# Another order of the source digits, source fields and bank clears in the set-up of a two-layer graph kernel, with the low-digit one-hots made on GpSimd

## The chip, the cores and the metric

The kernel runs on one core of one Trainium2 chip. The metric is the device time of one execution in microseconds (us). All numbers of the kernel before are from three timed runs and one further execution that the hardware profiler recorded.

Engines are called by these names in the rows: PE is TensorE's matrix multiply, PEld its weight load, DVE is VectorE, ACT is ScalarE, POOL is GpSimd, SP is SyncE, and a q behind a name is the queue of that engine (SPq issues most of the transfers).

## The reference

Two graph layers over 12,500 nodes with 128 features and 212,500 edges (100,000 drawn pairs in both directions and one loop for each node), sorted by target. Both have the form x = x + layer(relu(layernorm(x))).

```python
h = jnp.maximum(_layernorm(x, axis=-1), 0.0)
# layer 0
src_h = h[src] @ W_msg.T + b_msg
msg = src_h + edge_embed[jnp.clip(edge_type, 0, 8)]
messages = segment_sum(msg, dst)
x = x + gru_cell(messages, h)
h = jnp.maximum(_layernorm(x, axis=-1), 0.0)
# layer 1
agg = segment_sum(h[dst], src)
z = ((1.0 + eps) * h + agg) @ W1.T + b1
z = relu(batchnorm(z))
x = x + z @ W2.T + b2
```

Layer 0 sums over the targets, and layer 1 sums over the sources, though the edges are sorted by target. So the kernel must know for every edge where it would stand in an order by source.

## The kernel before

The nodes are cut into 98 blocks of 128, the edges into 1,664 tiles of 128. The program has one hand-written instruction list for each engine, and semaphores between them.

**Set-up.** It does three things side by side. (1) The first norm and the message table: 14 turns (LN_TURNS) of 7 blocks each. In a turn SP loads x (`load_x`), VectorE makes the statistics (`norm_stats`, `norm_scale`), ScalarE takes a root (`deviation`) and applies the norm (`norm0`), TensorE transposes (`hT`), ScalarE moves the result (`keep_hT`), TensorE multiplies by W_msg (`messages`), ScalarE moves it (`table_rows`), and SP writes it to the table in DRAM. Four buffers hold the loads. (2) The packed edges: target, source and type are packed into one word, written to DRAM, and read back with one tile in each column (semaphore `packed_in`). (3) The histogram of the sources: the high digit (13 values) and the low digit (8 values) of every edge's source block are turned into one-hot rows of bf16, in 13 pieces of 128 tiles (DPIECES), and TensorE multiplies the two one-hots of a piece (`digit_counts`, 16 multiplications) into bank 6. `digit_fields` takes the digits out of the packed words, and `digit_onehots(i)` makes the one-hots of piece i, in two buffers; piece i waits until TensorE has counted piece i-2. DIG_AT is the turn at which VectorE begins with the digits: from that turn on each turn also makes one piece, and the rest follow behind the last turn. TensorE counts a piece behind the transposes and messages of its turn, in the order of its list.

**From the histogram to the first gather.** When all 13 pieces are counted, VectorE reads bank 6, takes the source numbers out of the packed words, TensorE transposes them, ScalarE copies them to `srcI` (the first four of twelve `fields_moved`), and GpSimd copies 128 columns of them as offsets (`place_idx`) and begins to gather rows of the message table, one indirect transfer for each tile of 128 edges. Before its first gather GpSimd also waits until the message table is written (`tab_out`).

**The rest of the set-up on VectorE.** It makes the targets within a block (LOC), which ScalarE copies as fields 5 to 8; the first rows of each source block (`base_s`); the types (VAL, fields 9 to 12); the rows of `lastrow`, by which SP pads the last tiles; then `sblkE` and `skeyE`, block and key of each source, from `srcI`; and, at the head of layer 0, the first one-hots. Then `lastrow_set` lets SP write the padding rows.

**ScalarE behind the fields.** It clears the 7 fields' room and the rest of the sums Y (`zero_y`, in two parts; the second waits until VectorE has read the fields), then the two banks for the type counts (`counts_zero`) and four banks for the sums (`agg_zero`).

**Layer 0.** GpSimd issues 1,664 gathers into a ring of 8 slots of 4 tiles. SP relays: for each slot it tells TensorE that the rows have come (`tiles_in`) and, from the fourth on, tells GpSimd that a slot is free (`slot_free`), when the sums that read it are done. Between its first relays SP issues the padding rows and waits for each before the next (`pad_tiles`). TensorE multiplies each tile by a one-hot of its targets, VectorE adds the banks to Y. Then come the gated cell, layer 1 with 1,664 indirect scatters on GpSimd, and the last multiplications.

## Time and profile before

| | us |
|---|---|
| three timed runs, median | 4887.57 |
| lowest and highest | 4886.05 and 4891.22 |
| the profiled execution | 4883.31 |
| its span, first to last instruction | 4881.0 |
| GpSimd busy in the span | 3442.0 (71%) |
| TensorE busy | 3759.2 (77%) |
| VectorE busy | 2671.9 (55%) |
| ScalarE busy | 1613.8 (33%) |

The rows of the profile are read as follows. A row of the timeline has the start and the duration in us, the engine, the line in the kernel before, the operation, what it writes and what it reads, the shapes, and how many such instructions were merged; in brackets stand the idle time of the engine just before it and what ended that. A group of instructions has the total busy time, the mean in ns of one, and the idle time before all of them. The profiled execution is 4.26 us shorter than the median of the timed runs, and 2.31 us of it lie outside of the span.

### The profile page before, as it was taken

How to read it: one execution, taken by the hardware profiler on the slowest of the kernel's cores; microseconds unless marked ns; L12 is line 12 of the kernel's file. 1: busy time of each engine (PE TensorE's matmuls, PEld its weight loads, DVE VectorE, ACT ScalarE, POOL GpSimd, SP SyncE). 2: the span in 40 equal slices, each digit the busy share in tenths (PEclk: the TensorE clock that was granted, in tenths of full speed). 3: DMA queues.
4: the chain of work that ended last, by engine and by line, in shares of the span. 5: the costliest groups of instructions: out<-in, count | busy, mean ns of one | idle time of the engine just before them, and what ended most of it. 6: DMA issues, size and time to landing. Idle time of an engine off the chain costs nothing.

```text
span 4881.0 us, 93192 instructions
## 1 busy us (share of the span) xinstructions
PE 3759.2 (77%) x22928; PEld 2659.4 (54%) x23224; DVE 2671.9 (55%) x4808; ACT 1613.8 (33%) x3340; POOL 3442.0 (71%) x3576
## 2 busy tenths in 40 slices
PE   4698888888888888888787777777677775677457
PEld 3455555555555555556654444444466674667456
DVE  7777777777777777756821111111255552555267
ACT  4433333333333333333432222222222222222266
POOL 1577777777777777774167777777777777777763
PEclk8799988989899888999998999988888886788689
DMA  5332333333333221222222222222355553555365
GB/s 151 98 82 80 80 81 81 81 80 81 81 80 81 64 53 53 53 52 55 75 92 81 81 85 81 81 86 81 125 182 177 186 185 125 167 174 185 103 240 159
DMA packets 316351, 514.65 MB, mean 105 GB/s; under 512 B 73350, under 2 KB 231737, under 8 KB 300189
## 3 DMA queue, kind: packets, MB, share of 16 engines
q1 hardware_dynamic: 209245, 286.59, 18.6%
q0 software_dynamic: 106944, 226.05, 15.7%
q8 instruction: 83, 1.36, 0.1%
q14 instruction: 79, 0.65, 0.0%
HBM read 331.72 MB, written 180.64 MB: 105 GB/s over the span
## 4 chain that ended last, share of the span: by engine, by line
POOL 66%; issue 24%; PE 4%; DVE 2%; DMA 1%; POOLq 1%; ACT 1%; SPq 0%; ACTq 0%; DVEq 0%
POOL rows_by_src L692 34%; POOL sb_ring L662 31%; PE ps L1777 2%; DMA rows_by_src<-sb_cf 0%; PE ps L1797 0%; PE ps L1789 0%; POOL sb_oh L677 0%; DVE sb_stepE L966 0%; POOLq L157 0%; DMA rows_by_src<-sb_ring,sb_idxslot 0%; DVE sb_smalls L945 0%; ACT sb_ring L731 0%; DVE sb_stepE L969 0%; POOLq L689 0%; POOLq L153 0%
## 5 line engine op out<-in xcount | busy, mean ns | idle before, releaser
L692 POOL DMA_INDIRECT rows_by_src<-sb_ring,sb_idxslot x1664 | 1693.6, 1018 | 537.6 <-issue 503.8
L662 POOL DMA_INDIRECT sb_ring<-msg_table,sb_idxslot x1664 | 1584.9, 952 | 516.6 <-issue 504.1
L1593 PE MATMUL ps<-sb_zeros_b 128*128 128x512 bf16 x5465 | 1461.8, 416 | 105.2 <-issue 94.0
L1593 PEld LDWEIGHTS ps<-sb_zeros_b 128*128 128x128 bf16 x5760 | 580.8, 106 | 726.5 <-issue 284.2
L1733 PE MATMUL ps<-sb_H,sb_oh 128*128 x3520 | 616.1, 338 | 459.0 <-ACT ps L867 275.3
L1733 PEld LDWEIGHTS ps<-sb_H,sb_oh 128*128 128x128 f32 x3520 | 567.1, 245 | 562.3 <-issue 547.8
L1373 DVE TENSOR_SCALAR sb_oh<-sb_oh,sb_cf 128x512 f32<-128x512 bf16 x440 | 208.4, 501 | 1081.0 <-PE ps L1733 977.8
L791 ACT CAST sb_counts<-ps 54x512 bf16<-54x512 f32 x440 | 254.3, 578 | 1307.4 <-PE ps L1615 1294.8
L873 ACT CAST sb_ring<-sb_skeyE 128x4 f32 (+1 forms) x416 | 82.2, 198 | 1594.1 <-DMA rows_by_src<-sb_ring,sb_idxslot 1592.2
L1601 PEld LDWEIGHTS ps<-sb_ring,sb_oh 128*128 128x128 f32 x3520 | 504.5, 201 | 159.3 <-issue 95.9
L1601 PE MATMUL ps<-sb_ring,sb_oh 128*128 x3520 | 529.1, 292 | 41.4 <-SPq L476 41.1
L1230 DVE TENSOR_TENSOR sb_Y<-sb_Y,ps 128x512 f32 x440 | 300.8, 684 | 370.8 <-PE ps L1623 365.9
L1615 PE MATMUL ps<-sb_oh,sb_toh 128*54 128x128 bf16 x1760 | 244.8, 234 | 230.3 <-issue 214.4
L1198 DVE TENSOR_REDUCE sb_blks<-sb_blk1h 128x99 bf16<-128x396 bf16 x417 | 342.3, 821 | 0.0
L1217 DVE TENSOR_TENSOR sb_ranked<-ps,sb_blk1h 128x396 f32<-128x396 f32 x416 | 234.8, 564 | 183.6 <-PE ps L312 175.0
L1615 PEld LDWEIGHTS ps<-sb_oh,sb_toh 128*54 128x54 bf16 x1760 | 129.0, 106 | 326.5 <-issue 250.0
L1391 DVE TENSOR_TENSOR sb_Y<-sb_Y,ps 128x512 f32 x376 | 257.0, 684 | 69.0 <-PE ps L1746 57.1
L1381 DVE TENSOR_TENSOR sb_stepE<-sb_stepE,sb_cf 128x512 f32<-128x512 f32 x188 | 125.2, 686 | 285.6 <-PE ps L1746 285.4
L786 ACT CAST ps<-sb_zeros_b 54x512 f32<-54x512 bf16 x442 | 257.4, 582 | 14.1
L798 ACT CAST ps<-sb_zeros_b 128x512 f32<-128x512 bf16 x438 | 253.0, 578 | 12.3 <-DVE sb_Y L1230 12.3
L875 ACT COPY sb_ring<-ps 128x512 f32<-128x512 f32 x416 | 240.7, 579 | 36.6 <-PE ps L1733 36.6
L867 ACT CAST ps<-sb_zeros_b 128x512 f32<-128x512 bf16 x420 | 247.3, 589 | 13.3
(239 smaller groups left out, 4348.1 us busy)
## 6 DMA issues: line engine op xcount, KB each, us to landing
sb_stepE<-rows_by_src SPq DMA_DIRECT2D x110, 1088.0 KB
sb_oh<-step_targets SPq DMA_DIRECT2D x110, 512.0 KB, 3.9
rows_by_src<-sb_cf SPq DMA_DIRECT2D x588, 68.0 KB
sb_ring<-msg_table,sb_idxslot POOLq DMA_INDIRECT x1664
rows_by_src<-sb_ring,sb_idxslot POOLq DMA_INDIRECT x1664
sb_ring<-rows_by_src SPq DMA_DIRECT2D x15, 1088.0 KB, 5.1
msg_table<-sb_oh SPq DMA_DIRECT2D x14, 448.0 KB, 3.3
sb_oh<-in_x SPq DMA_DIRECT2D x49, 128.0 KB, 2.1
```

The lines of the kernel that those rows point to most:

```text
L662: pool.indirect_dma_start(out=ring[:, r * G + q, 0:F], out_offset=None, in_=table_d[:, :], in_offset=bass.IndirectOffsetOnAxis(ap=idxslot[ ...
L692: pool.indirect_dma_start(out=rows_d[:, :], out_offset=bass.IndirectOffsetOnAxis(ap=idxslot[:, h, g * G + q:g * G + q + 1], axis=0), in_=r ...
L786: return nc.scalar.copy(bank(5 + k)[0:TROWS, :], zeros_b[0:TROWS, :])
L791: nc.scalar.copy(counts[:, k, :], bank(5 + k)[0:TROWS, :]).then_inc(S("counts_moved"), 1)
L798: nc.scalar.copy(bank(1 + (g + 2) % G), zeros_b[:, :]).then_inc(S("agg_zero"), 1)
L1198: vs.tensor_reduce(blks[:, slot, :], own_blocks(slot).rearrange("p q b -> p b q"), axis=AX.X, op=ALU.add) \
L1230: vs.tensor_tensor(yb, yb, bank(1 + g), ALU.add).then_inc(S("agg_added"), 1)
L1391: vs.tensor_tensor(yb, yb, bank(GPC + g), ALU.add).then_inc(S("bank_free"), 1)
L1593: mm(o, zeros_b[:, 0:P], zeros_b[:, :], start=False, stop=True, skip_group_check=True)
L1601: mm(o, oh[:, k, s, :], ringf[:, ds(tile, F)], start=False, stop=True, skip_group_check=True)
L1615: m = mm(o, type_cols(k, s, q * HALVES // G), ohb[:, k, s, 1:2 * P:2], start=False, stop=True, skip_group_check=True)
L1733: m = mm(picked_ps[:, ds(slot, P)], pick[g][:, q * P:(q + 1) * P], H[:, ds(off, P)], start=False, stop=True, skip_group_check=True)
```

## The change

Four edits, all in the set-up.

1. DIG_AT goes from 3 to 6: VectorE begins with the digits three turns later, and TensorE's counts follow. Five pieces instead of two lie behind TensorE's last turn.
2. The low-digit one-hots move from VectorE (one TENSOR_TENSOR of 128x1024 for each piece) to GpSimd (eight TENSOR_SCALAR of 128x128 for each piece, one for each digit value, comparing with a constant and writing every eighth element), 104 instructions in all. They stand behind the 14 gathers of step tiles and ahead of the waits on the message table. `digits_set` starts them, and `hist_hi` and `hist_lo` take the place of `hist_oh`. The low digits are made in another buffer (`lo_dig`).
3. `sblkE` and `skeyE` are made ahead of the wait on fields 5 to 8, instead of behind `lastrow`.
4. ScalarE clears the count banks and the sum banks ahead of Y.

```diff
-DIG_AT = 3
+DIG_AT = 6
...
+            pool.wait_ge(S("digits_set"), 1)
+            for i in range(DPIECES):
+                wait(pool, "hist_ps", i - 1)
+                a = i * DPIECE
+                for h in range(NLO):
+                    o = nc.gpsimd.tensor_scalar(lo_oh[i % 2].rearrange("p (c h) -> p c h", h=NLO)[:, :, h],
+                                                lo_b[:, a:a + DPIECE], float(h), None, ALU.is_equal)
+                o.then_inc(S("hist_lo"), 1)
...
-            zero_y(3 * SW, Y.shape[1])
-            act.wait_ge(S("fields_read"), 1)
-            act.wait_ge(S("loc_out"), 16)
-            zero_y(0, 3 * SW).then_inc(S("y_zero"), 1)
...
             for g in range(G):
                 nc.scalar.copy(bank(1 + g), zeros_b[:, :]).then_inc(S("agg_zero"), 1)
+
+            zero_y(3 * SW, Y.shape[1])
+            act.wait_ge(S("fields_read"), 1)
+            act.wait_ge(S("loc_out"), 16)
+            zero_y(0, 3 * SW).then_inc(S("y_zero"), 1)
...
-                                 iota_b[:, 0:NHI].unsqueeze(1).to_broadcast([P, DPIECE, NHI]), ALU.is_equal)
-                vs.tensor_tensor(lo_oh[i % 2].rearrange("p (c h) -> p c h", h=NLO),
-                                 lo_b[:, a:a + DPIECE].unsqueeze(2).to_broadcast([P, DPIECE, NLO]),
-                                 iota_b[:, 0:NLO].unsqueeze(1).to_broadcast([P, DPIECE, NLO]), ALU.is_equal) \
-                    .then_inc(S("hist_oh"), 1)
+                                 iota_b[:, 0:NHI].unsqueeze(1).to_broadcast([P, DPIECE, NHI]), ALU.is_equal) \
+                    .then_inc(S("hist_hi"), 1)
...
-                link(vs.tensor_copy(hi_b, packed))
-                link(vs.tensor_scalar(packed, fldi[1][:, 0:TILES], 25, NLO - 1, ALU.logical_shift_right, ALU.bitwise_and))
-                link(vs.tensor_copy(lo_b, packed))
+                vs.tensor_copy(hi_b, packed)
+                link(vs.tensor_scalar(lo_dig, fldi[1][:, 0:TILES], 25, NLO - 1, ALU.logical_shift_right, ALU.bitwise_and))
+                vs.tensor_copy(lo_b, lo_dig).then_inc(S("digits_set"), 1)
+                dve.wait_ge(S("digits_set"), 1)
...
+            tmp = fldi[2][:, 0:TILES]
+            vs.memset(sblkE[:, TILES:TILES + G], 0.0)
+            link(vs.tensor_scalar(tmp, srcI, 7, None, ALU.logical_shift_right))
+            link(vs.tensor_copy(sblkE[:, 0:TILES], tmp))
+            link(vs.tensor_scalar(tmp, srcI, P - 1, None, ALU.bitwise_and))
+            link(vs.tensor_copy(skeyE[:, :], tmp))
 
             dve.wait_ge(S("starts_ps_s"), 1)
             dve.wait_ge(S("fields_moved"), 8)
...
-                pe.wait_ge(S("hist_oh"), i + 1)
+                pe.wait_ge(S("hist_hi"), i + 1)
+                pe.wait_ge(S("hist_lo"), i + 1)
```

On VectorE, where the digits begin: in the kernel before, the digits (L1095 to L1098) follow the statistics of turn 4, and a piece is one high and one low one-hot (L966, L969).

```order
L945 BN_STATS sb_smalls<-sb_ring 128x6 x7
L950 BN_AGGR sb_smalls<-sb_smalls 128x2 x7
L1095 TENSOR_SCALAR sb_Y<-sb_Y 128x1664
L1096 CAST sb_Y<-sb_Y 128x1664
L1097 TENSOR_SCALAR sb_Y<-sb_Y 128x1664
L1098 CAST sb_Y<-sb_Y 128x1664
L966 TENSOR_TENSOR sb_stepE<-sb_Y,sb_iota_b 128x1664
L969 TENSOR_TENSOR sb_stepE<-sb_Y,sb_iota_b 128x1024
L957 RECIPROCAL sb_smalls<-sb_smalls 128x7
```

In the changed kernel (whose lines are numbered about 10 higher) they follow the statistics of turn 7.

```order
L956 BN_STATS sb_smalls<-sb_stepE 128x6 x7
L961 BN_AGGR sb_smalls<-sb_smalls 128x2 x7
L1103 TENSOR_SCALAR sb_Y<-sb_Y 128x1664
L1104 CAST sb_Y<-sb_Y 128x1664
L1105 TENSOR_SCALAR sb_Y<-sb_Y 128x1664
L1106 CAST sb_Y<-sb_Y 128x1664
L977 TENSOR_TENSOR sb_stepE<-sb_Y,sb_iota_b 128x1664
L968 RECIPROCAL sb_smalls<-sb_smalls 128x7
```

The four digit instructions stand six statistics rows later, and the row of 128x1024 is gone from every piece.

On GpSimd, between the gathers of step tiles and the first offsets of layer 0, before:

```order
L619 COMPARE_AND_BRANCH
L617 UNCONDITIONAL_BRANCH
L635 DMA sb_Y<-packed_edges,sb_smalls 128x128 x14
L652 COPY sb_idxslot<-sb_stepE 128x128
L662 DMA sb_ring<-msg_table,sb_idxslot 128x128 x68
```

and now:

```order
L636 DMA sb_Y<-packed_edges,sb_smalls 128x128 x14
L645 ISA
L645 TENSOR_SCALAR sb_stepE<-sb_Y 128x128 x104
L662 COPY sb_idxslot<-sb_stepE 128x128
L672 DMA sb_ring<-msg_table,sb_idxslot 128x128 x68
```

The 104 comparisons stand directly ahead of the first gathers.

On VectorE behind the targets (the last cast of LOC), before:

```order
L1142 CAST sb_Y<-sb_Y 128x1792
L1149 CAST sb_Y<-ps 128x198
L1150 CAST sb_Y<-ps 128x99
L1151 TENSOR_SCALAR sb_Y<-sb_Y 128x297
L1153 TENSOR_TENSOR sb_Y<-sb_Y,sb_cf 128x297
```

and now:

```order
L1151 CAST sb_Y<-sb_Y 128x1792
L1154 MEMSET sb_sblkE 128x2
L1155 TENSOR_SCALAR sb_Y<-sb_stepE 128x1664
L1156 CAST sb_sblkE<-sb_Y 128x1664
L1157 TENSOR_SCALAR sb_Y<-sb_stepE 128x1664
L1158 CAST sb_skeyE<-sb_Y 128x1664
L1164 CAST sb_Y<-ps 128x198
```

The five instructions on the sources stand in front of the wait that L1149 (now L1164) begins with.

## Rows read from the trace of the kernel before

**Rows 1.** The page: busy time of each engine, and the chain that ended last.

```profile
PE 3759.2 (77%) x22928; PEld 2659.4 (54%) x23224; DVE 2671.9 (55%) x4808; ACT 1613.8 (33%) x3340; POOL 3442.0 (71%) x3576
...
POOL 66%; issue 24%; PE 4%; DVE 2%; DMA 1%; POOLq 1%; ACT 1%; SPq 0%; ACTq 0%; DVEq 0%
```

**Rows 2.** Groups of instructions on GpSimd: the scatters and the gathers.

```profile
L692 POOL DMA_INDIRECT rows_by_src<-sb_ring,sb_idxslot x1664 | 1693.6, 1018 | 537.6 <-issue 503.8 <-ACT sb_ring L875 33.8
L662 POOL DMA_INDIRECT sb_ring<-msg_table,sb_idxslot x1664 | 1584.9, 952 | 516.6 <-issue 504.1 <-SPq L480 11.7 <-POOL sb_idxslot L652 0.8
```

**Rows 3.** Timeline, 61 to 70 us: SP's queue and VectorE at the digits.

```profile
61.31 0.25 SPq L427 DMA_DIRECT2D sb_rowtab<-step_tables  x1
65.22 1.03 DVE L1095 TENSOR_SCALAR sb_Y<-sb_Y 128x1664 int32<-128x1664 int32 x1 [12.54 <-DMA sb_Y<-packed_edges]
...
69.47 1.89 DVE L966 TENSOR_TENSOR sb_stepE<-sb_Y,sb_iota_b 128x1664 bf16<-128x1664 bf16 x1
```

**Rows 4.** The line that loads x: time from issue to landing.

```profile
DMA to landing us min/median/max: 4.4/5.7/10.2
```

**Rows 5.** Timeline, 111 to 117 us: one turn on VectorE, and ScalarE's next norm.

```profile
111.33 0.19 DVE L957 RECIPROCAL sb_smalls<-sb_smalls 128x7 f32<-128x7 f32 x1
...
113.81 1.86 DVE L966 TENSOR_TENSOR sb_stepE<-sb_Y,sb_iota_b 128x1664 bf16<-128x1664 bf16 x1
...
115.59 1.22 DVE L969 TENSOR_TENSOR sb_stepE<-sb_Y,sb_iota_b 128x1024 bf16<-128x1024 bf16 x1
...
116.72 0.20 DVE L957 RECIPROCAL sb_smalls<-sb_smalls 128x7 f32<-128x7 f32 x1
...
117.15 2.80 ACT L731 ACTIVATE sb_ring<-sb_ring,sb_smalls 128x128 f32<-128x128 f32 x7 [0.71 <-DVE sb_smalls L959]
```

**Rows 6.** Timeline, 131 to 142 us: the last one-hot and the first gather.

```profile
131.60 1.22 DVE L969 TENSOR_TENSOR sb_stepE<-sb_Y,sb_iota_b 128x1024 bf16<-128x1024 bf16 x1
...
141.45 1.01 POOL L662 DMA_INDIRECT sb_ring<-msg_table,sb_idxslot  x1 [0.78 <-POOL sb_idxslot L652]
```

**Rows 7.** GpSimd's key one-hots at the kernel's end: ns min, median, max of one.

```profile
L711 POOL TENSOR_SCALAR sb_oh<-sb_cf,sb_ring x75: 593/601/1318, 4674.4 to 4817.6; 128x128 f32<-128x128 f32 x75
```

**Rows 8.** GpSimd's copies of offsets, in the same form.

```profile
L652 POOL COPY sb_idxslot<-sb_stepE x13: 288/299/306, 140.4 to 2004.5; 128x128 int32 x10, 128x128 int32<-128x128 int32 x3
```

**Rows 9.** Timeline of GpSimd, 4677 to 4698 us: two groups of five key one-hots.

```profile
4677.98 2.91 POOL L711 TENSOR_SCALAR sb_oh<-sb_cf,sb_ring 128x128 f32<-128x128 f32 x5 [0.29 <-PE ps L1777]
...
4693.41 3.87 POOL L711 TENSOR_SCALAR sb_oh<-sb_cf,sb_ring 128x128 f32<-128x128 f32 x5 [2.50 <-PE ps L1777]
```

**Rows 10.** Timeline of VectorE under the second of them.

```profile
4693.98 0.85 DVE L1427 TENSOR_TENSOR sb_H<-sb_H,sb_b2b 128x640 f32 x1
4695.10 0.56 DVE L1416 TENSOR_TENSOR sb_oh<-sb_ring,sb_cf 128x384 f32<-128x384 f32 x1 [0.26 <-issue]
...
4696.27 0.47 DVE L1416 TENSOR_TENSOR sb_oh<-sb_ring,sb_cf 128x256 f32<-128x256 f32 x1
```

**Rows 11.** Timeline, 155 to 189 us: VectorE, ScalarE and SP behind the first gather.

```profile
155.11 0.36 DVE L1149 CAST sb_Y<-ps 128x198 int32<-128x198 f32 x1 [3.88 <-ACT sb_stepE L770]
...
162.43 1.03 DVE L1175 TENSOR_SCALAR sb_Y<-sb_stepE 128x1664 int32<-128x1664 int32 x1
...
162.77 6.18 ACT L775 CAST sb_Y<-sb_zeros_b 128x7168 f32<-128x7168 bf16 x1
...
171.23 6.73 SPq L455 DMA_DIRECT2D rows_by_src<-sb_cf  x4
...
174.96 2.14 ACT L804 CAST ps<-sb_zeros_b 128x512 f32<-128x512 bf16 x4
...
188.33 0.69 DVE L1230 TENSOR_TENSOR sb_Y<-sb_Y,ps 128x512 f32 x1 [9.59 <-PE ps L1623]
```

**Rows 12.** Timeline of GpSimd, 188 to 201 us: the 32nd and the 33rd gather.

```profile
188.28 0.94 POOL L662 DMA_INDIRECT sb_ring<-msg_table,sb_idxslot  x1 [0.31 <-issue]
200.02 0.94 POOL L662 DMA_INDIRECT sb_ring<-msg_table,sb_idxslot  x1 [10.80 <-SPq L480]
```

7 lines of the change are left out of this document (1 added, 6 removed).

## The prediction, made before the changed kernel ran

> **What bounds the kernel now.** I read the page's busy times and its chain first. TensorE has more busy time than GpSimd, but the chain that ended last lies 66% on GpSimd, and the 24% called issue are mostly the gaps between its transfers [rows 1]. The groups of GpSimd say why: 1,664 gathers of 952 ns with 0.30 us between them (504.1 us of issue), and the same again for the scatters; in the whole of layer 0 GpSimd waited only 11.7 us for a free slot [rows 2]. So layer 0 ends about 1664 x 1.25 = 2080 us behind the moment from which GpSimd can gather without a stop, and what the set-up loses or saves ahead of that moment goes to the end one for one. Nothing later runs by an absolute date, so I count only the shift of that moment.
>
> That moment is not the first gather (141.45 [rows 6]). The 32 tiles of the ring are issued by 188.28, the 33rd could go at 188.28 + 1.25 = 189.5, and it goes at 200.02, released by SP's relay [rows 12]. The relay hangs on the padding rows that SP starts at 171.23, when VectorE has set `lastrow_set` [rows 11]: 28.8 us from there to the 33rd gather, with padding transfers one behind the other. The ring's date has 10.5 us of room, the relay's has none. Both dates come from the histogram: the first through SRC, TensorE and ScalarE, the second through VectorE's list. If the histogram ends D later, both move by D. So the shift at the end is D plus what the list between histogram and `lastrow_set` gains or loses.
>
> **Edit 3, the source fields.** VectorE is idle for 3.88 us in front of L1149, waiting for ScalarE's copies; the block that moves there is a small clear and four instructions of 1.03 us with hardly a gap, 4.3 us, and began at 162.43 [rows 11]. It reads `srcI`, which has been there since the first gather. In its new place it covers the idle time and passes it by 0.4 us. Removed 4.3, added 0.4: **3.9 us less** on the way to `lastrow_set`. What is late next is the ring's own date; of its 10.5 us of room 6.6 are left, so the whole 3.9 counts.
>
> **Edit 4, ScalarE's clears.** All the clears ended at 174.96 + 2.14 = 177.1 [rows 11]. In the new order the banks are clear first and Y last, at about the same time, for the work is the same and the wait on `fields_read` is met earlier. Y is first needed by VectorE's add at 188.33 [rows 11], in the new kernel 3.9 earlier, 184.4 on the old scale. Cover of 7 us, so nothing; the cleared banks let TensorE start its first counts earlier, and then it waits for the relay all the same. Without that cover each us of late clear would cost one. Nothing.
>
> **Edit 1, the digits three turns later.** Before, VectorE stood idle 12.54 us for the packed words and started the digits at 65.22, the first one-hot at 69.47; they take 4.25 us [rows 3]. Now it goes on with the norm meanwhile. The digits follow the statistics of turn 7. These need x of turn 7, and SP issues that load behind the table loads that end at 61.31 + 0.25, and one table write: at about 62.0. Its landing takes 5.7 us in the median [rows 4]: 67.7. Statistics take 2.1 (of the 2.48 from 111.33 to 113.81, without the scale's 0.38 [rows 5]): 69.8. Digits: 4.25. So `digits_set` comes at **74.0**, 4.5 us later than the first one-hot began before, but with three turns more of the norm done.
>
> From there a turn would be quick: it took 5.39 us (111.33 to 116.72), of which the low one-hot is 1.13 (115.59 to 116.72), so VectorE needs 4.26; ScalarE waited 0.71 in it, so ScalarE needs 4.68 [rows 5]. Were GpSimd free of cost, the histogram would end thus: first high one-hot 75.9, seven turns of 4.7 to 108.8, five pieces of 1.89 behind them to 118.3, against 131.60 + 1.22 = 132.8 before [rows 6]. D would be -14.5. That is the best case.
>
> **Edit 2, GpSimd's 104 comparisons.** They are in a row with the histogram: the last piece cannot be counted before they are done. A piece costs 8d + L: d is the time of one comparison, L what VectorE takes from GpSimd.
>
> d has no row. The nearest above is GpSimd's key one-hot: the same operation on as many elements, but with a scalar from a tensor for each partition and 32-bit data; 601 ns in the median [rows 7], and 2.91 / 5 = 0.58 us from start to start [rows 9]. The nearest below is its copy of 128 elements, 299 ns [rows 8], with neither comparison nor scalar. The new instruction has the comparison, a constant in the place of the tensor's scalar, and bf16 written with a step of eight. I see no reason to set it at either end and take the middle, **d = 0.44**, with 0.30 and 0.58 for the range.
>
> L: five key one-hots took 2.91 us alone and 3.87 when VectorE ran three TENSOR_TENSORs with both inputs in SBUF, 0.85 + 0.56 + 0.47 us [rows 9, 10]. That is 0.96 lost in 1.88, or each of them less 0.3. The high one-hot is such an instruction too and takes 1.86 [rows 5]: L = 1.86 - 0.3 = **1.56**. Bounds: 0, and 1.86.
>
> The Trainium skill (SBUF — State Buffer, "Who interferes with whom") says that a VectorE instruction with two SBUF inputs and a GpSimd instruction that reads SBUF exclude each other for the whole instruction. The rows agree in kind and fall 0.3 us short of it in size; by the rule alone the sum below would be 13 x 0.3 = 3.9 us longer.
>
> Sum: 74.0 + 13 x (8 x 0.44 + 1.56) = 74.0 + 66.0 = 140.0. A piece of 5.08 us is longer than ScalarE's 4.68, so GpSimd sets the pace, and the norm's turns follow it, because TensorE counts a piece between two turns. The message table is done well ahead: five pieces, 25 us, lie behind its last turn. D = 140.0 - 132.8 = +7.2. **Net: 7.2 - 3.9 = +3.3 us.** The profiled execution would go from 4883.31 to 4886.6. The median lies 4.26 above the profiled one, and I keep that distance: 4887.57 + 3.3 = 4890.9. A measurement of this kernel can tell about 0.2%, 9.8 us, from no change.
>
> **Rivals.**
> - *GpSimd's comparisons cost as much as the key one-hots* (slower). With d = 0.58 and L = 1.56: 13 x 6.20 = 80.6, end 154.6, D = +21.8, net +17.9: 4905.5. With L = 1.86 net +21.8: 4909.4. It decides from 8d + L = 4.82 on (d = 0.41), and is over 0.2% from 5.58 on (d = 0.50). For it: the same operation and element count [rows 7]. Against it: no scalar to fetch, half the bytes.
> - *GpSimd is hidden under the turns* (faster). If 8d + L stays under 4.7, the norm's turns set the pace and D is -14.5, net -18.4: 4869.2. That wants d under 0.39 with L = 1.56, or a small L. Over 0.2% faster is reached at 8d + L = 4.07. For it: the copy's 0.30 [rows 8] would give 3.96 a piece.
> - *The move does not reach the end.* If something else than the histogram sets the 33rd gather, as the ring's own date, all that is left is noise about 4887.6. Against it: 10.80 us of idle time that SP ended [rows 12].
>
> The Trainium skill (GPSIMD Engine Reference, 3.1) gives about 1.8 cycles for an element at 1.2 GHz in the best case: an estimate of 0.19 us for 128 elements and the dispatch on top, near the copy's end. By it the second rival would come true. The key one-hots of this trace take three times as long, so it holds here for the copy at most, and no run yet shows which way the new instruction goes.
>
> **How the numbers follow.** Chances: the forecast, a piece between 4.1 and 5.6 us, 0.44; slower rival 0.34; faster rival 0.20; no reach 0.02, which counts as within. So faster by over 0.2% 0.20, within 0.46, slower 0.34. The best case's 4869.2 asks that every turn runs at ScalarE's pace and loads never wait; I leave the last part of it out, and take the slower rival with both its values of L in: 4875 to 4909.
>
> **What would show it right or wrong.** In the changed kernel's timeline: `digits_set` at 74, the 104 comparisons with start to start near 0.44 us and a stop of about 1.6 at each high one-hot; the last count near 141; the first gather near 149; VectorE's source block directly behind LOC with no idle time of 3.9 in front of L1164; the 33rd gather near 203, still released by SP. Wrong would be a comparison at 0.3 or at 0.6, VectorE's one-hots not holding GpSimd at all, x loads that bring `digits_set` past 78, or a first add of VectorE that waits for Y.

## The result, and the profile after

| | kernel before | changed kernel |
|---|---|---|
| median, us (range) | 4891.22 (4886.05 to 4894.47) | 4921.63 (4911.25 to 4931.17) |
| ratio, 95% interval | | 1.0062 (1.0048 to 1.0077) |
| profiled execution: time / span | 4883.31 / 4881.0 | 4922.07 / 4919.6 |
| 104 comparisons: first start to last end | | 74.46 to 186.54 |
| first gather | 141.45 | 195.89 |
| 33rd gather | 200.02 | 250.40 |
| last gather / first scatter / last scatter | 2244.9 / 2456.1 / 4658.0 | 2294.5 / 2503.3 / 4695.9 |

The change costs 0.6%, some 30 us. The forecast was 4890.9 with a range up to 4909: the sign of the small loss was right, its size was not, and the time is outside the range.

GpSimd's groups in the changed kernel (line, operation, count, then busy us and mean ns, then idle time before them and who ended it), and one line's summary (ns min/median/max):

```profile
L702 POOL DMA_INDIRECT rows_by_src<-sb_ring,sb_idxslot x1664 | 1684.1, 1012 | 536.5 <-issue 503.5 <-ACT sb_ring L886 32.9
L672 POOL DMA_INDIRECT sb_ring<-msg_table,sb_idxslot x1664 | 1584.0, 952 | 512.7 <-issue 502.6 <-SPq L481 9.3 <-POOL sb_idxslot L662 0.8
L645 POOL TENSOR_SCALAR sb_stepE<-sb_Y 128x128 bf16<-128x128 bf16 x104 | 107.9, 1189 | 24.6 <-DVE sb_Y L1106 20.4
```

```profile
L645 POOL TENSOR_SCALAR sb_stepE<-sb_Y x104: 984/987/2685, 74.5 to 185.6; 128x128 bf16<-128x128 bf16 x104
```

The gathers are what they were, the scatters 9.5 us shorter in all [rows 2]; the third group is new. Its timeline, with the gathers behind it:

```profile
74.46 112.08 POOL L645 TENSOR_SCALAR sb_stepE<-sb_Y 128x128 bf16<-128x128 bf16 x104 [20.40 <-DVE sb_Y L1106]
...
195.89 1.20 POOL L672 DMA_INDIRECT sb_ring<-msg_table,sb_idxslot  x1 [0.81 <-POOL sb_idxslot L662]
```

```profile
242.63 0.94 POOL L672 DMA_INDIRECT sb_ring<-msg_table,sb_idxslot  x1 [0.30 <-issue]
250.40 0.94 POOL L672 DMA_INDIRECT sb_ring<-msg_table,sb_idxslot  x1 [6.82 <-SPq L481]
```

The comparisons start where the forecast put them (74.0), but take 112.08 us in place of 66.0: 8.62 us a piece, not 5.08. The histogram's last piece ends at 186.54, where before it ended at 132.82 [rows 6]: D is +53.7, not +7.2. Who waited for them (engine and line, whom it waited for, us in total, times, longest):

```profile
PE ps L1534 <- POOL sb_stepE L645: 62.8, 13, 9.3
DVE sb_stepE L977 <- PE ps L1534: 60.3, 11, 6.8
```

The whole histogram now walks at GpSimd's pace. VectorE's high one-hots stand 8.67 us apart, with 6.8 us idle before each, and its first step behind the histogram waits 13.87:

```profile
163.85 1.89 DVE L977 TENSOR_TENSOR sb_stepE<-sb_Y,sb_iota_b 128x1664 bf16<-128x1664 bf16 x1 [6.78 <-PE ps L1534]
172.52 1.89 DVE L977 TENSOR_TENSOR sb_stepE<-sb_Y,sb_iota_b 128x1664 bf16<-128x1664 bf16 x1 [6.78 <-PE ps L1534]
```

```profile
188.28 0.36 DVE L1122 TENSOR_TENSOR sb_ranked<-ps,sb_cf 104x192 f32<-104x192 f32 x1 [13.87 <-PE ps L1534]
```

Edits 3 and 4 did what the forecast said. The source block fills VectorE's idle time, and the line that had waited 3.88 us [rows 11] now follows it with no wait:

```profile
208.90 1.03 DVE L1158 CAST sb_skeyE<-sb_Y 128x1664 bf16<-128x1664 int32 x1
210.04 0.36 DVE L1164 CAST sb_Y<-ps 128x198 int32<-128x198 f32 x1
```

ScalarE clears the banks, then Y; the padding rows start at 222.14, and VectorE's first add into Y waits for TensorE, long after Y is clear (232.2):

```profile
218.89 2.13 ACT L809 CAST ps<-sb_zeros_b 128x512 f32<-128x512 bf16 x4
220.97 6.16 ACT L785 CAST sb_Y<-sb_zeros_b 128x7168 f32<-128x7168 bf16 x1
...
231.81 0.40 ACT L787 CAST sb_Y<-sb_zeros_b 128x256 f32<-128x256 bf16 x1
```

```profile
222.14 7.56 SPq L456 DMA_DIRECT2D rows_by_src<-sb_cf  x4
```

```profile
240.71 0.69 DVE L1239 TENSOR_TENSOR sb_Y<-sb_Y,ps 128x512 f32 x1 [14.39 <-PE ps L1633]
```

So +53.7 and -3.9 should make +49.8 at the 33rd gather, and it came +50.4. From here on the account has a second hole: the last gather is +49.6, but the last scatter only +37.9, and the medians differ by 30. The scatters of the kernel before and of the changed one (ns min/median/max, first and last start):

```profile
L692 POOL DMA_INDIRECT rows_by_src<-sb_ring,sb_idxslot x1664: 963/967/3222, 2456.1 to 4658.0; - x185
L702 POOL DMA_INDIRECT rows_by_src<-sb_ring,sb_idxslot x1664: 954/958/3212, 2503.3 to 4695.9; - x185
```

Each is 9 ns shorter, at the least and in the median. Two questions: why is a comparison so dear, and where do some 15 to 20 us come back?

### The profile page after: what moved, and what is told of

Its sections match the earlier page's. It is cut to its first block, busy times and chain, and to the rows that moved or that the text cites. A ratio compares the mean times of both kernels' runs of the same rounds, so it can differ in the third digit from the quotient of the medians.

```text
span 4919.6 us, 93236 instructions
## 1 busy us (share of the span) xinstructions
PE 3767.8 (77%) x22928; PEld 2675.2 (54%) x23224; DVE 2661.0 (54%) x4795; ACT 1616.1 (33%) x3340; POOL 3535.9 (72%) x3680
## 4 chain that ended last, share of the span: by engine, by line
POOL 67%; issue 24%; PE 4%; DMA 2%; DVE 1%; POOLq 1%; SPq 1%; ACT 1%; ACTq 0%; DVEq 0%
POOL rows_by_src L702 34%; POOL sb_ring L672 30%; PE ps L1787 3%; POOL sb_stepE L645 2%; DMA rows_by_src<-sb_cf 1%; PE ps L1807 0%; PE ps L1799 0%; DMA rows_by_src<-sb_ring,sb_idxslot 0%; POOL sb_oh L687 0%; SPq L463 0%; PE ps L1603 0%; POOLq L157 0%; POOLq L699 0%; POOLq L153 0%; SPq L464 0%
## 5 line engine op out<-in xcount | busy, mean ns | idle before, releaser
L1625 PE MATMUL ps<-sb_oh,sb_toh 128*54 128x128 bf16 x1760 | 244.9, 234 | 223.0 <-issue 214.3
```

The costliest lines, as they stand in the source:

```text
L1625: m = mm(o, type_cols(k, s, q * HALVES // G), ohb[:, k, s, 1:2 * P:2], start=False, stop=True, skip_group_check=True)
```

## Experiments on the price of a comparison

**Taken apart at the end of GpSimd's list.** The kernel before, with comparisons and copies added behind its last key one-hots:

```diff
+            for h in range(8):
+                gt.tensor_scalar(d8[0][:, :, h], src, float(h), None, EQ)      # bf16, step 8
+            for k in range(4):
+                gt.tensor_scalar(ringf[:, 1024 + k * P:1024 + (k + 1) * P], iota_f, iota_p, None, EQ)
...
+            for k in range(4):
+                gt.tensor_scalar(tb[:, 3072 + k * P:3072 + (k + 1) * P], src, 3.0, None, EQ)
+            for h in range(8):
+                gt.tensor_scalar(d8[1][:, :, h], src, 7.0 if h < 4 else 0.0, None, EQ)
...
+            for k in range(3):
+                gt.tensor_scalar(rb[:, k * 512:(k + 1) * 512], skeyE[:, 0:512], 3.0, None, EQ)
```

> The kernel before with a row of small instructions at the end of GpSimd's list, behind its last key one-hots, where VectorE runs nothing with two SBUF inputs. In order: 8 comparisons exactly as in the changed kernel (bf16, constants 0 to 7, columns 0 to 7 with step 8); 4 as the key one-hots (f32, scalar from a tensor, dense); 4 f32 dense with a constant; 4 bf16 dense with a constant; 8 bf16 with step 8, where the constant is 7 for columns 0 to 3 and 0 for columns 4 to 7; 4 f32 with step 8; 3 bf16 dense of 512 elements; 8 copies bf16 with step 8; 4 copies bf16 dense. Their results are used by nothing. Theory A (the write with a step makes the cost): bf16 dense 0.6 us or less, both step-8 groups near 1.05 from start to start, the f32 one with step 8 too. Theory B (a comparison with a constant or in bf16 costs it): bf16 dense near 1.05 too, and the copies at 0.3 in either pattern. Either way the first group shows whether columns 4 to 7 cost more than 0 to 3 (0.60 against 1.05 in the changed kernel), and the fifth whether that goes with the column or with the constant.

GpSimd's timeline:

```profile
4832.11 7.08 POOL L723 TENSOR_SCALAR sb_oh<-sb_skeyE 128x128 bf16<-128x128 bf16 x8 [7.34 <-PE ps L1814]
4839.27 2.35 POOL L725 TENSOR_SCALAR sb_ring<-sb_cf 128x128 f32<-128x128 f32 x4
4841.59 2.02 POOL L727 TENSOR_SCALAR sb_ring<-sb_cf 128x128 f32<-128x128 f32 x4
4843.56 2.02 POOL L729 TENSOR_SCALAR sb_oh<-sb_skeyE 128x128 bf16<-128x128 bf16 x4
4845.64 7.07 POOL L731 TENSOR_SCALAR sb_oh<-sb_skeyE 128x128 bf16<-128x128 bf16 x8
...
4854.35 4.46 POOL L735 TENSOR_SCALAR sb_ring<-sb_skeyE 128x512 bf16<-128x512 bf16 x3
```

Eight of the change's comparisons, with no other engine near, take 7.1 us: 0.88 each, as in the changed kernel. The key one-hot's own form takes 0.58 here (L725: 2.32 to the next group, four of them), a constant in place of the tensor's scalar 0.49 (L727), and bf16 in place of float32 changes nothing as long as the values are written side by side (L729: 0.49 between starts). So type and scalar are innocent; the write with a step of eight is part of it. Singly, the starts of L723 are 0.60 apart for constants 0 to 3, 1.10 from 3 to 4, and 1.06 from 4 on. L731 exchanged the constants over the columns, and the gaps went with the constants, not with the columns.

**Constant, data or place in the list.** Other constants and data in the same spot: eight with 3, eight with 7, four side by side with 7, eight from another row with 7 and 3, four of step 4 and two of step 2, eight that ask "not less than".

```diff
+            for h in range(8):
+                gt.tensor_scalar(d8[0][:, :, h], src, 3.0, None, EQ)
+            for h in range(8):
+                gt.tensor_scalar(d8[1][:, :, h], src, 7.0, None, EQ)
+            for k in range(4):
+                gt.tensor_scalar(rb[:, k * P:(k + 1) * P], src, 7.0, None, EQ)
+            for h in range(8):
+                gt.tensor_scalar(d8[2][:, :, h], iota_f, 7.0 if h < 4 else 3.0, None, EQ)
...
```

> The kernel before with 38 comparisons of 128 elements at the end of GpSimd's list, after its last key one-hots: nothing else waits for them but the end of the program. The first probe left open what makes a comparison that writes bf16 at every eighth place take 0.60 us or 1.06 us: constants 0 to 3 gave 0.60 and constants 4 to 7 gave 1.06, in whatever column. Eight with constant 3 (all columns), eight with constant 7 (all columns), four dense ones with constant 7, eight of step 8 from a float32 row with constants 7 and 3, four of step 4 and two of step 2 with 7 and 3, eight that ask for 'not less than' 7 and 3. Theory C (the constant itself): constant 3 gives 0.60 eight times and constant 7 gives 1.06 eight times, and 7 is dearer than 3 in the step-8 groups with other data and other operation too. Theory M (what the data hold, the number of ones written): the float32 row, in which each value stands once in every partition, gives one time for 7 and 3 alike, and 'not less than' turns the order round. Theory P (the place in the list, four cheap and four dear ones): both groups of eight show four and four. The dense ones with constant 7: 0.49 if the step is needed for the dear form, about 0.9 if not. Time: that of the kernel before plus about 25 us.

```profile
6272.95 5.34 POOL L724 TENSOR_SCALAR sb_oh<-sb_skeyE 128x128 bf16<-128x128 bf16 x8 [7.34 <-PE ps L1811]
6278.35 8.39 POOL L726 TENSOR_SCALAR sb_oh<-sb_skeyE 128x128 bf16<-128x128 bf16 x8
6286.80 2.30 POOL L728 TENSOR_SCALAR sb_ring<-sb_skeyE 128x128 bf16<-128x128 bf16 x4
```

and single instructions at the passage from constant 7 to constant 3 and on to the next group, which begins with 7:

```profile
6292.33 0.99 POOL L730 TENSOR_SCALAR sb_oh<-sb_cf 128x128 bf16<-128x128 f32 x1
6293.38 0.99 POOL L730 TENSOR_SCALAR sb_oh<-sb_cf 128x128 bf16<-128x128 f32 x1
6293.98 0.99 POOL L730 TENSOR_SCALAR sb_oh<-sb_cf 128x128 bf16<-128x128 f32 x1
...
6295.18 1.04 POOL L730 TENSOR_SCALAR sb_oh<-sb_cf 128x128 bf16<-128x128 f32 x1
6296.28 0.70 POOL L732 TENSOR_SCALAR sb_ring<-sb_skeyE 128x128 bf16<-128x128 bf16 x1
```

Theory C holds: eight with constant 3 take 5.34 us, eight with constant 7 take 8.39, whatever they are compared with; the float32 row and "not less than" show the same gaps. Data and place are out. The lines also say what the expected text had not seen: one comparison of step 8 takes 0.99 to 1.15 us whatever its constant; with constants up to 3 the next one starts before it has ended, 0.60 behind, and if either of two neighbours is a 7 it starts only after the end. The step sets the size: with 7 the gap is 0.59 side by side (with 3 it was 0.49, so a 7 costs 0.10 even there), 0.63 at step 2, 0.77 at step 4 and 1.06 at step 8. Why a constant should matter is not explained by anything here. (This ran on another chip, on which the whole kernel is slower; more on that below. GpSimd's instructions take the same time on it.)

**The same comparisons in place, written side by side.** GpSimd writes each comparison's 128 values as neighbours, and TensorE reads them with a step instead:

```diff
-                    o = nc.gpsimd.tensor_scalar(lo_oh[i % 2].rearrange("p (c h) -> p c h", h=NLO)[:, :, h],
+                    o = nc.gpsimd.tensor_scalar(lo_oh[i % 2][:, h * DPIECE:(h + 1) * DPIECE],
...
-                           lo_oh[i % 2][:, a * DW:(a + 1) * DW], start=False, stop=True, skip_group_check=True)
+                           lo_oh[i % 2].rearrange("p (h c) -> p c h", h=NLO)[:, a * DCOLS:(a + 1) * DCOLS, :],
+                           start=False, stop=True, skip_group_check=True)
```

> The changed kernel, but GpSimd writes each comparison densely (128 elements of one digit value behind the other) and TensorE reads them with a step of 128; the counts are the same. Theory A (the write with a step): a comparison about 0.6 us, a piece 8 x 0.6 + 1.6 = 6.4 us in the place of 8.62, the last comparison near 158 in the place of 186.5, and 28 us faster than the changed kernel, so about at the time of before. Theory B (the instruction itself costs 1 us): no difference from the changed kernel, some 30 us slower than before.

```profile
75.05 79.27 POOL L645 TENSOR_SCALAR sb_stepE<-sb_Y 128x128 bf16<-128x128 bf16 x104 [21.09 <-DVE sb_Y L1106]
...
164.08 1.20 POOL L672 DMA_INDIRECT sb_ring<-msg_table,sb_idxslot  x1 [0.81 <-POOL sb_idxslot L662]
```

79.27 us in place of 112.08: 6.10 a piece. The step alone costs the change 33 us. Yet the 33rd gather is still 18.9 us later than in the first profile of the kernel before (218.91), and the time, 4888.2 against 4892.3 (ratio 0.9995, 0.9986 to 1.0005), shows none of it: the second hole again.

## Experiments on the other edits

**Edit 3 alone** (the source block moved in the kernel before, as in the diff of the change):

> The kernel before with the block of source fields in its new place and nothing else. If the relay's date sets the 33rd gather: first gather unchanged at 141.5, 33rd gather at 196.1 in the place of 200.0, 3.9 us faster (0.08%). If the ring's own date or something behind it sets the pace, the 33rd gather stays at 200 and there is no difference.

**Edits 1, 3 and 4, without edit 2** (VectorE makes both one-hots):

```diff
-            pool.wait_ge(S("digits_set"), 1)
-            for i in range(DPIECES):
...
+                vs.tensor_tensor(lo_oh[i % 2].rearrange("p (c h) -> p c h", h=NLO),
+                                 lo_b[:, a:a + DPIECE].unsqueeze(2).to_broadcast([P, DPIECE, NLO]),
+                                 iota_b[:, 0:NLO].unsqueeze(1).to_broadcast([P, DPIECE, NLO]), ALU.is_equal) \
+                    .then_inc(S("hist_oh"), 1)
```

> The changed kernel with the low one-hots back on VectorE (edits 1, 3 and 4 alone). If GpSimd's comparisons are the whole loss: digits_set at 74, seven turns of 5.4 us and five pieces of 3.1 behind them, last low one-hot near 130 against 132.8 before, the 33rd gather near 193 (200.0 minus 2.8 minus 3.9), and 7 us faster than before. If the later start of the digits costs by itself (rival): last low one-hot at 140 or later and no gain.

The first gives 4885.19 (0.9989, 0.9979 to 0.9999), the second 4885.06 (0.9981, 0.9972 to 0.9991), against 4892.3. Their 33rd gathers stand at 194.16 and 195.02, 5.9 and 5.0 us earlier than in the first profile of the kernel before. But that date moves by itself. On the same chip as these two, the kernel before with the comparisons at its end, whose set-up is untouched, had its 33rd gather here:

```profile
197.93 0.95 POOL L662 DMA_INDIRECT sb_ring<-msg_table,sb_idxslot  x1 [9.41 <-SPq L480]
```

Against it the two are 3.8 and 2.9 us earlier. So edit 3 is worth its 3.9 us, and edits 1 and 4 add nothing that shows, in the date or in the time, whose intervals overlap: the change is a small gain with its second edit left out.

**The digits two turns later than before, one earlier than in the change** (`DIG_AT = 5`, the rest as in the last one):

> Edits 3 and 4 with both one-hots on VectorE and the digits before the norm scale of turn 5 (DIG_AT 5): one turn earlier than in the kernel with edits 1, 3 and 4, where the last low one-hot came at 129.4 and the first gather at 139.9. The one-hots then start where the load of the packed rows has just landed. Expected: last low one-hot at 127 to 129, first gather at 138 to 140, and the median 5 to 10 us under the kernel before, 0 to 3 under that with DIG_AT 6. Rival (the wait for the load stalls VectorE's norm turns): 0 to 3 over it.

```profile
65.13 1.03 DVE L1097 TENSOR_SCALAR sb_Y<-sb_Y 128x1664 int32<-128x1664 int32 x1 [0.32 <-DMA sb_Y<-packed_edges]
```

The packed words have just landed when VectorE comes to the digits (0.32 us idle in place of 12.54 [rows 3]), and the norm of two more turns is done. The 33rd gather comes at 192.18, 4882.87 against 4889.86 (0.9984, 0.9975 to 0.9993). The last low one-hot starts at 126.18 and the first gather at 136.67, against 129.40 and 139.88 with `DIG_AT` at 6 (on another chip): by these dates the best place for the digits is where their data arrive, and the change had passed it by a turn. The two times do not tell them apart.

**Edit 1 undone in the changed kernel:**

```diff
-DIG_AT = 6
+DIG_AT = 3
```

> The changed kernel with DIG_AT at 3 again, so edit 1 undone and the rest kept. My theory (comparisons on GpSimd set the end, and edit 1 only moves their start): the comparisons start at about 69.4 us in place of 74.5, last as long (112 us), and the 33rd gather comes at about 245 in place of 250.4; the whole about 5 us under the changed kernel, 4916 if that measures 4921. Rival (edit 1 costs something else, in the order of VectorE and the source fields): the gain is over 10 us. Rival (the first gather's delay does not reach the end one to one): under 2 us.

**The changed kernel again,** on the same chip as that one:

> The changed kernel once more, beside the kernel before and the padded one on one chip. Expected: 25 to 32 us over the kernel before; first gather at 196, 33rd at 250, scatters at least 954 ns again if that belongs to the program, 954 or 963 if it is chance. If theory L of the padded kernel holds, the changed kernel is 48 to 52 us over the padded one (the whole shift of the 33rd gather, 50.4 us); if not, about 30 over both.

```profile
74.41 112.71 POOL L645 TENSOR_SCALAR sb_stepE<-sb_Y 128x128 bf16<-128x128 bf16 x104 [20.35 <-DVE sb_Y L1106]
```

```profile
79.90 112.71 POOL L645 TENSOR_SCALAR sb_stepE<-sb_Y 128x128 bf16<-128x128 bf16 x104 [25.93 <-DVE sb_Y L1106]
```

The first line is the one with `DIG_AT` at 3, the second the changed kernel: 5.5 us between the starts, 5.2 between the 33rd gathers (257.11 and 262.30), and 7 us between the medians (6396.12 and 6403.07). Once GpSimd sets the pace, three turns of patience are three turns lost: with edit 2 in the kernel, edit 1 makes the 33rd gather about 5 us later. The times agree with that but do not show it, with five executions each that spread over 20 us.

**Every second piece on GpSimd,** written side by side, with `DIG_AT` at 5:

```diff
+POOL_PIECES = (1, 3, 5, 7, 9, 11)
...
-            for i in range(DPIECES):
+            for i in POOL_PIECES:
                 wait(pool, "hist_ps", i - 1)
```

> Edits 3 and 4, DIG_AT at 5, and GpSimd makes the low-digit one-hots of every second piece only (1, 3, ... 11), each comparison writing 128 neighbouring values, with TensorE reading them at a step of 128; VectorE makes the other seven. A piece costs GpSimd 6.1 us at the rate of the dense kernel, and two pieces go by in 9 to 10 us, so GpSimd should keep up and VectorE be rid of 6 x 1.56 = 9.4 us. Theory A: last low one-hot at 121 to 124, first gather at 131 to 134, 33rd at 186 to 189, the median 11 to 16 us under the kernel before. Rival (the comparisons are needed before GpSimd has them, or its held port slows the norm turns): first gather at 138 or later, no better than the kernel with edits 3 and 4 and VectorE's one-hots.

```profile
83.17 6.06 POOL L646 TENSOR_SCALAR sb_stepE<-sb_Y 128x128 bf16<-128x128 bf16 x8 [5.11 <-PE ps L1542]
91.39 8.08 POOL L646 TENSOR_SCALAR sb_stepE<-sb_Y 128x128 bf16<-128x128 bf16 x8 [2.16 <-PE ps L1542]
```

The rival held in part. Five of the six pieces take GpSimd 8.1 to 9.0 us in place of 6.1, with two or three of VectorE's one-hots beside each; the second, which has only one beside it, takes 6.06. TensorE waits for the last of them until 133.5. The first gather comes at 145.36, 11 us and more later than hoped. Still the time is 4876.57 against 4889.86 (0.9963, 0.9950 to 0.9976), with the 33rd gather only 2.4 us earlier: the second hole once more.

## Experiments on what came back

**A first gather that is late for no other reason.** The kernel before, with 500 memsets of one element ahead of the first gather:

```diff
             pool.wait_ge(S("fields_moved"), 4)
+            for j in range(5):
+                for k in range(100):
+                    o = nc.gpsimd.memset(spare[:, k:k + 1], 0.0)
+                o.then_inc(S("spare_set"), 1)
+                pool.wait_ge(S("spare_set"), j + 1)
```

> The kernel before with 500 memsets of one element a partition at 0.102 us (51 us) on GpSimd between its last wait and the first gather: nothing of the change, only a first gather that comes some 52 us later. Theory A (what set-up adds ahead of the gathers is carried to the end whole): first gather at 193, 33rd at 246 to 250, the median 46 to 50 us over the kernel before on a chip like that of the first job. Then what the changed kernel lost less than its own 50 us (30 us timed, with scatters of 954 in place of 963 ns) is due to something in edit 2 that the padded kernel did not have. Theory B (a later start is partly made up in the steps behind it, whatever made it late): the median only 25 to 38 us over.

```profile
143.09 16.09 POOL L674 MEMSET sb_spare<- 128x1 bf16 x475 [0.24 <-issue]
```

```profile
206.49 0.94 POOL L663 DMA_INDIRECT sb_ring<-msg_table,sb_idxslot  x1 [3.03 <-SPq L481]
```

The memsets are far cheaper in a row than I took them to be: 16.09 / 475 = 0.034 us. The first gather is 19.6 us late, the 33rd 6.5, and the ratio is 1.0009 (1.0000 to 1.0018), +4.4 us. The expected 50 us were missed. The run still shows that the first gather has room, as the prediction said. The time agrees with the 33rd gather's 6.5 us reaching the end (theory A), but so small a delay cannot tell that from a part of it. The profiles can: from the 33rd to the last gather it is 2043.8 to 2048.2 us in every kernel on the chips of the 4890 us kind, whenever the 33rd came.

**The changed kernel beside it:**

> The changed kernel beside the late one: first gather at 196, 33rd at 250 (on a chip like the first job's), scatters at least 954 ns. Theory A: 8 to 20 us under the late kernel (the shorter scatters' 15 us). Theory B: within 5 us of it, both 25 to 38 over the kernel before.

4924.98 against 4889.86: 1.0067 (1.0054 to 1.0080), +32.8 us, with the 33rd gather at 252.52, +52.5. The difference of about 20 us is there again, so theory A holds as far as the last gather, and something in edit 2 gives time back behind it.

**Is it the number of instructions on GpSimd's list?** 104 memsets behind the step tiles' transfers, in GpSimd's idle time:

```diff
+            for k in range(DPIECES * NLO):
+                nc.gpsimd.memset(spare[:, k:k + 1], 0.0)
```

> The kernel before with 104 GpSimd memsets of one element a partition, into a buffer that nobody reads, where the changed kernel has its 104 comparisons (behind the step tiles' DMAs, in time in which GpSimd idles). In the kernel with dense comparisons the 33rd gather came 18.9 us later than in the kernel before, and the time was 4 us shorter; there and in the changed kernel every scatter took 954 ns at the least, in the four profiles whose GpSimd has no comparisons 963 ns. Theory L (what stands ahead on GpSimd's list makes the scatters 9 ns shorter, 15 us for 1664): the first and the 33rd gather as before (141 and 200 us), the scatters' least time 954 ns, and the median 10 to 15 us under the kernel before. Theory R (chance from execution to execution, or the comparisons' later start): scatters at 963 ns and the median within 4 us of the kernel before.

**Is it their kind?** One comparison in that place; 104 comparisons of one element; one addition:

```diff
+            nc.gpsimd.tensor_scalar(spare[:, 0:104], iota_f[:, 0:104], 3.0, None, ALU.is_equal)
```

> The kernel before with one comparison of 104 float32 elements (a new buffer that nobody reads) on GpSimd behind the step tiles' DMAs, at about 55 us, in time in which GpSimd idles. Open: in the first job's and the third job's kernels whose GpSimd list begins with comparisons (the changed one, the dense one, the split one) every scatter takes 954 ns at the least and GpSimd's key one-hots some 5% less (692 for 730 ns), and the timed median lies 11 to 23 us under what the 33rd gather's move gives; 104 memsets in the same place did not do that (965 ns on the second chip, where the changed kernel had 956). Theory K (the first comparison's kind of instruction, run before the gathers, is what changes the scatters, one is enough): scatters at 954 ns, key one-hots at 692, median 12 to 18 us under the kernel before. Theory N (the number of comparisons, or the smaller VectorE list of the changed kernel, does it): 963 ns, 730 ns, median within 4 us of the kernel before.

```diff
+            for k in range(DPIECES * NLO):
+                nc.gpsimd.tensor_scalar(spare[:, k:k + 1], iota_f[:, k:k + 1], 3.0, None, ALU.is_equal)
```

> The same with 104 comparisons of one element a partition, as many instructions of that kind as the changed kernel has. Theory K: the same as with one, 954 ns and 12 to 18 us under the kernel before. If the number decides: this one shows 954 and the one with a single comparison 963. If neither shows it, the cause lies outside GpSimd's list (VectorE's or TensorE's part of edit 2).

```diff
+            nc.gpsimd.tensor_tensor(spare[:, 0:104], iota_f[:, 0:104], iota_f[:, 0:104], ALU.add)
```

> The same with one addition of two tensors (104 float32 elements) in place of the comparison. If any arithmetic instruction ahead of the gathers does it: 954 ns and 12 to 18 us. If it must be the comparison's kind: 963 ns and within 4 us of the kernel before.

The scatters of these four (ns min/median/max, first and last start), in the order 104 memsets, one comparison, 104 comparisons, addition:

```profile
L696 POOL DMA_INDIRECT rows_by_src<-sb_ring,sb_idxslot x1664: 965/971/1679, 3093.4 to 6095.7; - x185
```

```profile
L696 POOL DMA_INDIRECT rows_by_src<-sb_ring,sb_idxslot x1664: 952/958/1667, 3135.1 to 6222.2; - x185
```

```profile
L697 POOL DMA_INDIRECT rows_by_src<-sb_ring,sb_idxslot x1664: 952/958/1667, 3149.7 to 6247.6; - x185
```

```profile
L696 POOL DMA_INDIRECT rows_by_src<-sb_ring,sb_idxslot x1664: 962/967/1670, 3162.9 to 6246.2; - x185
```

A comparison ahead of the gathers shortens each later scatter by 10 ns, memsets and an addition do not (the changed kernel had 956 on the chip of the memsets). Only comparisons were tried, no other operation of the same instruction. With the single comparison the gathers became longer, and with 104 of them they did not:

```profile
L666 POOL DMA_INDIRECT sb_ring<-msg_table,sb_idxslot x1664: 946/952/2461, 147.3 to 2898.5; - x185
```

```profile
L667 POOL DMA_INDIRECT sb_ring<-msg_table,sb_idxslot x1664: 938/944/2448, 146.6 to 2913.1; - x185
```

The key one-hots did not follow, against the expected text: the mean of the 75 that read the ring stays at 730 to 734 ns here (730 before), where the kernels whose low one-hots GpSimd makes have 692 to 694. So that is a side effect of its own, and it is worth nothing at the end: behind the last scatter the span has 223.7 us in the changed kernel and 223.0 before.

The times could not show the worth of the shorter scatters here: all four ran on chips on which GpSimd does not set the pace (see the last section). They were 6326.4 against 6327.39 for the memsets, and against 6444.83 there were 6440.6 for one comparison, 6459.19 for 104 (1.0023, 1.0011 to 1.0035, slower) and 6445.23 for the addition.

**One comparison on top of the kernel with `DIG_AT` 5:**

> The kernel with edits 3 and 4, DIG_AT 5 and VectorE's one-hots (7.0 us under the kernel before in the last job) with the one comparison on GpSimd added. Theory K: both gains add, 19 to 25 us under the kernel before, some 4868. Theory N: 5 to 9 under it, as without the comparison.

6441.61 against 6444.83, 0.9989 (0.9976 to 1.0002), on the same slow chip; scatters 956, gathers 949. The expected 19 to 25 us did not come, and by the waits of that chip (last section) the time can say nothing of chips on which GpSimd sets the pace.

**The 104 small comparisons again, where GpSimd sets the pace:**

> The kernel before with 104 comparisons of one element a partition on GpSimd in its idle time at 55 us, again, on what may be a chip like those of the first and third job, where GpSimd sets the scatter phase. On the last chip its scatters took 952 ns at the least and its gathers 938, against 962 and 938 in the kernel with an addition in that place. If such a comparison is what shortened the changed kernel's scatters: 952 to 954 ns, and 12 to 18 us under the kernel before on a chip on which that takes about 4890 us; on a slow chip (6300 us and more) TensorE and ScalarE set the scatter phase and no gain is expected (within 15 us). If it is not: 963 ns and within 4 us.

```profile
54.32 25.80 POOL L642 TENSOR_SCALAR sb_spare<-sb_cf 128x1 f32<-128x1 f32 x104
```

```profile
L697 POOL DMA_INDIRECT rows_by_src<-sb_ring,sb_idxslot x1664: 954/958/3607, 2455.0 to 4643.9; - x185
```

4874.12 against 4891.27, 0.9969 (0.9957 to 0.9981): 104 comparisons whose result nobody reads, in time in which GpSimd waits, make the kernel 15 to 17 us faster (by the ratio and by the medians), although its 33rd gather is 2.1 us later. Memsets and an addition were not timed on a chip of this kind; that they would gain nothing here rests on their scatters of 962 to 965 ns.

**The same with edits 3 and 4 and `DIG_AT` 5:**

> Edits 3 and 4, DIG_AT 5, both one-hots on VectorE, and the 104 small comparisons on GpSimd. If both gains add, on a chip of the 4890 us kind: 33rd gather at 192, scatters at 952 to 954, and 19 to 25 us under the kernel before (4865 to 4871). If only the set-up's part counts: 5 to 9 under it.

33rd gather at 190.14, 4867.66 against 4891.27: 0.9953 (0.9940 to 0.9967), 23 us faster than the kernel before and over 50 faster than the changed one. The two gains add up (-7.8 and -15.2 alone). It is the best version of this case.

All the kernels on chips of the 4890 us kind, side by side. The dates are taken against the first profile of the kernel before (200.02), the last column but one is the measured ratio's loss or gain in us, with an interval of 4 to 7 us to either side, and the last one what of it the 33rd gather does not explain:

| kernel | 33rd gather against before | least scatter, ns | time against before, us | rest |
|---|---|---|---|---|
| edit 3 | -5.9 | 963 | -5.4 | +0.5 |
| edits 1, 3, 4 | -5.0 | 963 | -9.3 | -4.3 |
| edits 3, 4, DIG_AT 5 | -7.8 | 963 | -7.8 | 0.0 |
| late first gather | +6.5 | 963 | +4.4 | -2.1 |
| changed kernel | +50.4 | 954 | +30.3 | -20.1 |
| changed kernel, again | +52.5 | 954 | +32.8 | -19.7 |
| comparisons side by side | +18.9 | 954 | -2.4 | -21.3 |
| every second piece | -2.4 | 954 | -18.1 | -15.7 |
| 104 small comparisons | +2.1 | 954 | -15.2 | -17.3 |
| the same, edits 3, 4, DIG_AT 5 | -9.9 | 954 | -23.0 | -13.1 |

The rest is near zero where a scatter takes 963 ns at the least (mean -1.5) and -13 to -21 where it takes 954 (mean -17.9). 1664 scatters, 9 ns shorter, make 15.0 us, and the two groups lie 16.4 apart, the same within their intervals. (Three of the kernels, edit 3, edits 1, 3, 4 and comparisons side by side, ran on the chip with 197.93 for the kernel before; with that date their rests are -1.6, -6.4 and -23.4, and the groups lie 15.7 apart.)

A single profile can hide this. In that of the changed kernel's second run on such a chip the first and the last scatter are 2201.7 us apart, as in the kernel before (2201.9), though its median scatter is 958 ns. About a hundred scatters in each execution take longer than 1.1 us, and what the long ones take beyond 1 us goes from 70 to 95 us in the ten profiles of the table and the one before; it was 93 in that one and 80 before. The gain stands in the least and the median scatter and in the medians of many executions, and need not stand in the sum of one.

## Why the prediction was wrong

- **The bound.** Right: GpSimd's gathers start the clock for layer 0, and the 33rd one, behind SP's relay, is the date that counts; each kernel of the table bears it out, the late first gather above all.
- **Edit 3.** Right: -3.9 forecast, and alone it made the 33rd gather 3.8 us earlier than in the kernel before on the same chip (5.9 against the first profile, of which about 1 us was an earlier last one-hot in that execution).
- **Edit 4.** Right as far as shown: no run has it alone, and Y was clear 8.5 us before the first add.
- **Edit 1.** Right in its date (74.0 forecast, 74.46, 75.05 and 75.41 in three profiles, and 79.90 on a slower chip, past the 78 that was to be a sign of being wrong) and wrong in its worth. With GpSimd in front the date is all there is, and it is 5 us worse. With VectorE's one-hots the last low one-hot ended at 130.62 in place of 132.82, a gain of 2 us.
- **Edit 2, the term L.** Right: 1.56 forecast. The last piece, beside which VectorE runs no one-hot, takes 7.0 us, and the mean piece 8.62: 1.6 lost to the high one-hot. The Trainium skill (SBUF — State Buffer, "Who interferes with whom") says that the two exclude each other for the whole instruction; the high one-hot takes 1.89, so the runs come 0.3 us short of the rule here as well.
- **Edit 2, the term d.** This is the step that failed: 0.44 us, range 0.30 to 0.58; it was 0.88. By the prediction's own formula, 74.46 + 13 x (8 x 0.88 + 1.6) = 186.8, and the trace has 186.54. The 1.6 comes from the same trace, the 0.88 also from the probe, and it makes 45.8 of the 46.5 us by which D was missed: the whole miss in set-up is this one term. The bounds did not bound: the key one-hot was called the nearest row above, though it writes its values side by side, and the new instruction's step of eight was named as a difference but given no price. The probes price what I weighed: constant for tensor scalar -0.09, bf16 for float32 nothing, a constant of 7 in place of 3 +0.10 side by side, step of eight +0.11 with constants up to 3 and another +0.47 with 7.
- The Trainium skill (GPSIMD Engine Reference, 3.1) gives about 1.8 cycles as the best case for an element, at 1.2 GHz 1.5 ns. This case's comparison is not that case: from 128 to 512 elements it goes from 0.49 to 1.44 us from start to start (L729, and L735 to the next group at 4858.68), 2.5 ns for an element. The measurement decides.
- **The slower rival** had the right mechanism, "it decides from 8d + L = 4.82 on", and a piece of 8.6 was past any value that it allowed.
- **The faster rival** was priced too well. Its D of -14.5 asks that GpSimd cost nothing; with the 13 pieces in a row, as the sum has them, a piece of 4.7 gives 74.0 + 61.1 = 135.1, a D of +2.3. So the lower end of the range, 4875, had less behind it than the text says. This did not cause the miss.
- **One for one to the end.** Right for the gathers, and incomplete: the prediction counted "only the shift of that moment" and had no term for a later phase that becomes quicker. Edit 2 has such a side effect of about -15 us, which no row of the kernel before shows. With d at 0.88 the forecast would have been 4887.57 + 53.0 - 3.9 = 4936.7, 15 us too long, and the change itself, +49.1 in place of +30.3, 19 us too dear.

## What to carry to other kernels

Before work moves to GpSimd, price its exact form, with the step of its output and its constants, and not the nearest relative: 128 bf16 values cost from 0.49 to 1.06 us between starts here, and a split over two engines runs at the slower one's pace, and pays on top what they take from each other. When data arrive late, put their use at the turn in which they arrive, neither earlier nor later (12.54 us idle with `DIG_AT` 3, 0.32 with 5, and a first gather 3.2 us later with 6). And when a kernel's time moves by less than its critical date, compare the least and the median time of the long repeated groups in both profiles: 9 ns in 1664 instructions took back 15 us here and left a loss of 30.
